# Attention block on one core: values and denominators side by side on TensorE, the tail's row operations parted, the tail's loads moved

## The reference

```python
mod = (silu(c) @ w_mod)                       # rows sa, ca, ga, sb, cb, gb for each batch
h = layernorm(x) * (1 + ca) + sa
q, k, v = split(h @ W_qkv + b_qkv)            # 16 heads of 32 channels
q, k = rope(q), rope(k)
p = softmax(causal(q @ k.T / sqrt(32)))
x = x + ga * ((p @ v) @ W_proj + b_proj)
h = layernorm(x) * (1 + cb) + sb
x = x + gb * (layernorm(h + outs) * ln_g + ln_b)
```

## Time and profile before

| | us |
|---|---|
| median of 3 runs | 3283.07 (3282.28 to 3283.45) |
| the profiled execution | 3289.78 |
| its span, first to last instruction | 3288.0 |
| PE busy | 3013.8 (92%) |
| DVE busy | 2501.4 (76%) |
| ACT busy | 1849.9 (56%) |
| POOL busy | 1588.9 (48%) |

### The profile page before, as it was taken

One profiled execution on the slowest core, in us unless ns is written; L12 is line 12 of the kernel. 1 busy time (PEld: TensorE's weight loads), 2 busy tenths in 40 slices (PEclk: granted clock), 3 DMA queues, 4 the chain that ended last, 5 costly groups with the idle time before them and its releaser, 6 DMA issues.

```text
span 3288.0 us, 59164 instructions
## 1 busy us (share of the span) xinstructions
PE 3013.8 (92%) x21664; PEld 1155.9 (35%) x21664; DVE 2501.4 (76%) x4214; ACT 1849.9 (56%) x3651; POOL 1588.9 (48%) x1586
## 2 busy tenths in 40 slices
PE   3799999999989999999998999999998999999896
PEld 1324343434343433434333242433324343242222
DVE  4697777777768788777877878777886878878477
ACT  3416565786655554785455555587545555455541
POOL 2303434482616465382644726365471645627355
PEclk8759999999999999999999999999999999999997
DMA  5403030413041220413113041311314122031122
GB/s 210 107 6 70 11 75 14 101 39 76 14 104 40 61 66 24 98 43 86 39 47 100 27 95 33 80 54 42 83 36 114 39 56 59 30 75 46 55 74 65
DMA packets 180875, 205.27 MB, mean 62 GB/s; under 512 B 21460, under 2 KB 137428, under 8 KB 179428
## 3 DMA queue, kind: packets, MB, share of 16 engines
q1 hardware_dynamic: 180584, 201.50, 23.4%
HBM read 114.09 MB, written 36.50 MB: 46 GB/s over the span
## 4 chain that ended last, share of the span: by engine, by line
PE 46%; issue 19%; DVE 16%; POOL 6%; POOLq 5%; DVEq 3%; ACT 3%; DMA 1%; SPq 1%; ACTq 1%
PE ring L1147 10%; PE ps_out L1197 9%; DVE mpart L902 9%; PE ps_scores L1183 7%; PE ps_scores L1121 5%; PE ps_den L1214 4%; PE ps_den L1220 3%; PE ring L1169 3%; POOL psum L529 3%; PE ps_scores L1133 2%; POOL psum L528 2%; DVE wk L948 1%; DVE dsum L918 1%; DVE wk L946 1%; POOLq L502 1%
## 5 line engine op out<-in xcount | busy, mean ns | idle before, releaser
L730 ACT ACTIVATE prob<-ps_scores 128x512 f32<-128x512 f32 (+3 forms) x2560 | 1257.8, 537 | 981.9 <-PE ps_scores L1186 477.2
L902 DVE TENSOR_REDUCE mpart<-ring 128x1 f32<-128x512 f32 (+3 forms) x2560 | 1403.1, 599 | 344.4 <-PE ring L1147 179.5
L1147 PE MATMUL ring<-qk 96*128 96x512 f16 (+3 forms) x2560 | 876.7, 365 | 73.6 <-DVE mpart L902 56.3
L1183 PE MATMUL ps_scores<-qk 98*128 98x512 f16 (+3 forms) x2560 | 867.2, 352 | 55.7 <-ACT prob L730 28.4
L528 POOL TENSOR_TENSOR psum<-prob 128x512 f32<-128x512 f32 x360 | 481.7, 1338 | 391.9 <-ACT prob L730 299.9
L1197 PE MATMUL ps_out<-prob,v 128*32 128x512 f32 (+3 forms) x5120 | 607.6, 547 | 0.0
L1147 PEld LDWEIGHTS ring<-qk 96*128 96x128 f16 x2560 | 236.1, 98 | 887.3 <-DVE mpart L902 625.2
L529 POOL TENSOR_TENSOR psum<-prob 128x512 f32<-128x512 f32 x360 | 483.4, 1343 | 0.0
L1183 PEld LDWEIGHTS ps_scores<-qk 98*128 98x128 f16 x2560 | 247.1, 99 | 370.1 <-ACT prob L730 215.7
L1121 PE MATMUL ps_scores<-hT,wg 128*128 128x512 f16 x1536 | 345.6, 382 | 3.5 <-POOL hT L519 3.5
L547 POOL TENSOR_TENSOR xs<-xs,bc 128x512 f32<-128x512 f32 x60 | 77.4, 1289 | 383.4 <-DMA xs<-in_L_attn_x_dram 382.1
(11 more groups left out here) (126 smaller groups left out, 2719.7 us busy)
## 6 DMA issues: line engine op xcount, KB each, us to landing
qk<-half SPq DMA_DIRECT2D x384, 128.0 KB, 3.6
turn<-in_rope_dram SPq DMA_DIRECT2D x64, 512.0 KB, 4.7
xs<-in_L_attn_x_dram SPq DMA_DIRECT2D x124, 256.0 KB, 2.8
attn_out_T<-ot SPq DMA_DIRECT2D x63, 256.0 KB, 2.2
otin<-attn_out_T SPq DMA_DIRECT2D x30, 512.0 KB, 4.8
out_dram<-x SPq DMA_DIRECT2D x60, 256.0 KB, 2.1
wg<-w_qkv_halves SPq DMA_DIRECT2D x16, 768.0 KB, 5.6
qk<-in_L_wmod_dram SPq DMA_DIRECT2D x1, 6144.0 KB, 26.8
```

Of the source, the lines that this page charges most:

```text
L730: act.activation(prob[:, s % 3, p, h % 2, 0:w], ps_scores[(HG * s + h) % NBK][:, 0:w], ACT.Exp, scale=SCALE).then_inc(exp_done, 1)
L902: dve.tensor_reduce(mpart[:, h, qt, kc:kc + 1], ring[use % NBK][:, 0:w], AX.X, ALU.max).then_inc(ring_free, 1)
L1147: mm = pe.matmul(ring[use % NBK][:, 0:w], qk[0:R, G % 2, 0, h, qt * P:(qt + 1) * P], qk[0:R, G % 2, 1, h, kc * QC:kc * QC + w], start=True ...
L1183: mm = pe.matmul(ps_scores[k % NBK][:, 0:w], qk[0:RM, par, 1, h, kt * P:(kt + 1) * P], qk[0:RM, par, 0, h, cq * QC + q0:(cq + 1) * QC], st ...
```

## The change

PE: V moves from place 2 to place 3 in every step, right ahead of D. The order becomes S0 U0 S1 U1 S2 U2 S3 V D U3 U4. DVE: of the two row operations of stages 2 and 4 only the first stays in its place; the second comes after the maxima of U2 and U3. U2's maximum also goes ahead of the reciprocals of parts 0 and 2, U3's ahead of those of parts 1 and 3. SP: the six rows of a new batch are loaded in chunk 0, and the first tail tile's load goes behind the rope load and behind the stacking of chunk 2's queries.

```diff
             def qkv(G, before, row_load, tail_load):
                 for c in range(NC_):
                     if c > 0:
                         stack_halves(G, c - 1, 1)
-                    if c == 2:
-                        tail_load()
                     if G < NG * B - 1 or c < NC_ - 1:
                         load_turn(NC_ * G + c + 1)
                     if c == 0 and before is not None:
                         maxima_rows(before, before % 2)
+                    if c == 0:
+                        row_load()
                     stack_halves(G, c, 0)
+                    if c == 2:
+                        tail_load()
                 stack_halves(G, NC_ - 1, 1)
...
+            def rows_load(b):
+                sp.wait_ge(tail_done, wait_value(NT * b))
+                sp.wait_ge(mod_st, 32)
+                sp.dma_start(bc[:], mod_d[b, 2:8, :].rearrange("(a m) n -> a m n", a=1).to_broadcast(
+                    [P, 6, C])).then_inc(bc_ld, 16)
+
             def tail_loads(b, t, xs_use, count):
                 Z = NT * b + t
-                if t == 0:
-                    sp.wait_ge(tail_done, wait_value(Z))
-                    sp.wait_ge(mod_st, 32)
-                    sp.dma_start(bc[:], mod_d[b, 2:8, :].rearrange("(a m) n -> a m n", a=1).to_broadcast(
-                        [P, 6, C])).then_inc(bc_ld, 16)
...
+                    def row_load():
+                        if 0 in tail.values():
+                            rows_load(b - 1)
...
                     dve.wait_ge(tail_rstd1, Z + 1)
                     dve.scalar_tensor_tensor(wk[:, i, :], x1[:, i, :], mv[:, i, 0:1], bc[:, 2, :], ALU.subtract, ALU.mult)
+                elif stage == 3:
                     dve.drain()
-                    dve.scalar_tensor_tensor(wk[:, i, :], wk[:, i, :], rstd[:, i, :], bc[:, 3, :], ALU.mult, ALU.add)
-                    dve.drain()
-                elif stage == 3:
                     dve.bn_stats(stats[:, i, :], wk[:, i, :])
...
                 else:
-                    tail_third(b, t)
+                    dve.wait_ge(tail_rstd2, Z + 1)
+                    dve.scalar_tensor_tensor(wk[:, i, :], wk[:, i, :], mv2[:, i, 0:1], bc[:, 4, :], ALU.subtract, ALU.mult)
+
+            def tail_second_row(b, t, stage):
+                i = t % 2
+                dve.drain()
+                if stage == 2:
+                    dve.scalar_tensor_tensor(wk[:, i, :], wk[:, i, :], rstd[:, i, :], bc[:, 3, :], ALU.mult, ALU.add)
+                else:
+                    dve.wait_ge(tail_x1_shift, NT * b + t + 1)
+                    dve.scalar_tensor_tensor(x1[:, i, :], wk[:, i, :], rstd2[:, i, :], xs[:, i, :], ALU.mult,
+                                             ALU.add).then_inc(tail_done, 1)
...
                                 tail_stage(b - 1, tail[s - 2 * stage], stage)
-                        out_parts(G, g, s, (0, 2), first, bool(own))
                         for u, h in units[2:3]:
                             unit_max(h, u, n)
                             n += 1
+                        out_parts(G, g, s, (0, 2), first, bool(own))
+                        for u, h in units[3:4]:
+                            unit_max(h, u, n)
+                            n += 1
+                        for stage in (2, 4):
+                            if s - 2 * stage in tail:
+                                tail_second_row(b - 1, tail[s - 2 * stage], stage)
...
-                            if place == (3 if s > 1 and STEPS[s - 1][1] == 0 else 2) and s > 0:
+                            if place == 3 and s > 0:
                                 values(G, par, s - 1, nxt)
-                            if place == 3 and s > 0:
                                 denominators(G, s - 1, nxt)
```

More of the change, by code:

```diff
@@ L359, in stack_halves, with qkv @@
                                  half[:, kind, a, :]).then_inc(stack_dma[kind], 16)
-            def qkv(G, before, tail_load):
+            def qkv(G, before, row_load, tail_load):
                 for c in range(NC_):
@@ L426, in body @@
                     else:
-                        qkv(NG * b + g + 1, NG * b + g, lambda: tail_load(FIRST_TAIL))
+                        qkv(NG * b + g + 1, NG * b + g, row_load, lambda: tail_load(FIRST_TAIL))
                     if not (last and g >= NG - 2):
@@ L440, in body @@
                             store_out(b - 1, tail[s - 9])
+                        if s + 2 in own and own[s + 2] == 0:
+                            rows_load(b)
                         if s + 2 in own:
@@ L467, in _ @@
             load_turn(0)
-            qkv(0, None, lambda: None)
+            qkv(0, None, lambda: None, lambda: None)
             load_group(1)
@@ L1035, in body @@
                         out_parts(G, g, s, (1, 3), first, bool(own))
-                        for u, h in units[3:]:
+                        for u, h in units[4:]:
                             unit_max(h, u, n)
```

## The result

The kernel after takes 3288.07 us (median of 14 runs, 3283.67 to 3291.99), the kernel before, run beside it on the same chip, 3281.03 (14 runs, 3277.34 to 3285.09). The ratio is 1.0022 [1.0015, 1.0030]: 7 us slower, where 62 us faster was forecast. The two profiled executions stand closer together: the span fell from 3288.0 to 3286.4, because the one of before lies 8.7 us above its later median and that of after (3288.19) does not. What follows goes group by group, and against more than one run of the same order.

A forecast was written before the change was run, and what follows sets the result against it. PE, busy 92% of the span, was taken to bound the kernel, with POOL nearly as hard in tail stretches. Terms -12 + 18 - 54 - 18 + 4 = -62 gave 3228, less 6.7 for the median: 3221 us, 8-in-10 range 3172 to 3268.

The forecast's parts named there:

- groups 0, 1, 3: Attention-only groups, PE idle 1.7 us only: V and D joined save 4 us a group, -12 in all.
- head groups: Groups 2, 6, 10: odd steps wait for the head's bank, other joins give back 2.4; +6 us each, +18.
- nine tail groups: Groups with tail tiles: joins and shorter waits for DVE give -6 us each, -54 (nothing to -10 each).
- loads: First projection phase of a new batch: rope load ahead of the tile removes waits, -18 us (-22 to -8).
- last group: No U between S0 and S3, so full-width steps wait on ACT: +0.17 in 21 steps, +4 us (-4 to +8).
- Joins where PE decides: Groups 0, 1, 3: each V-D join saves 0.24 us of PE, 24 joins a group, taken as -4 a group.
- Odd head steps: Groups 2, 6, 10: U2 waits for ACT to empty the head's bank, V and D behind it; +0.88 in 14 steps.
- stretches under POOL's pace: Tail-group stretches full of POOL's additions, half the joins: PE gains at most POOL's idle 8.1 us, taken as 2.
- joins outside: Tail-group joins outside the stretches full of POOL's additions: 13 at 0.24 us save 3.1 a group.
- waits for DVE: Tail groups: the 1.28 us before step 24's projection and some smaller waits go, 2 us a group.
- The first rival, POOL's pace: Locked ports and full POOL stretches leave 1 us a tail group in place of 6: -17, 3266 us; chance 0.14.
- Second rival, U2 too early: U2 ahead of V waits for its bank in every step with a D: +42 at w = 0.3, 3325 us; chance 0.11.

The follow-up runs named there:

- the rows alone: The kernel before with only DVE's parted row operations and earlier maxima: 3273.14 us, ratio 0.9976, 6.7 us faster.
- with POOL light: Kernels before and after, each with POOL's pair additions over 128 of 512 columns: 3210.82 and 3217.09 us.
- the tile's place mended: The kernel after with the first tail tile's load moved behind the stacking of chunk 2's keys: 3261.76 us, ratio to before 0.9945.
- the order alone: The kernel before with only the new place of V on PE: 3306.41 us, ratio 1.0077, 27 us slower.
- the loads alone: The kernel before with only SP's moved loads: 3278.04 us, ratio 0.9996.
- where it pays 3: After with selective V-D joins, statistics ahead of U3's maximum, later first tail tile load and addition, head tiles' loads ahead of columns and weights: 3223.09 us, ratio to before 0.9823.
- the three versions with the later tile: After with the first tail tile's load behind chunk 2's key stacking, alone or with two sets of further edits: 3261.76, 3238.11 and 3223.09 us.

## Why the prediction was wrong, step by step

The terms, forecast and as the profiles have them (the second from the same group lengths and step lengths as above):

| term | forecast | profile |
|---|---|---|
| groups 0, 1, 3 | -12 | -12.4 |
| head groups | +18 | +22.9 |
| nine tail groups, steps 2 to 39 | -54 | -15 |
| loads: steps 0 and 1 of tail groups, projection phases | -18 | +1.5 |
| last group | +4 | +2.7 |
| sum | -62 | about 0 |

The sum goes with the two profiles, whose spans differ by -1.6. The medians differ by +7, because the execution of before that was profiled is an unusually long one: its group 7 alone stands 5 above groups 11 and 14. So the -15 of the tail groups flatters the change; some 10 is likelier, an estimate from those three groups.

- *Joins where PE decides*: right for the group, 4.1 with 4 forecast. Of the 24 newly joined steps of group 1, 13 save 0.23 to 0.25, the size read from the earlier trace rows, and 130.7 us is the length in every run with all of these joins.
- *Odd head steps*: right in place and size. Step 27 of group 2 in after, for comparison with the earlier trace rows:

```profile
693.71 0.38 PE L1207 MATMUL ps_scores<-qk 98*128 98x512 f16 x1
695.30 0.39 PE L1171 MATMUL ring<-qk 96*128 96x512 f16 x1 [1.21 <-ACT x L773]
695.52 0.38 PE L1207 MATMUL ps_scores<-qk 98*128 98x512 f16 x1
695.84 1.07 PE L1221 MATMUL ps_out<-prob,v 128*32 128x512 f32 x8
696.72 1.04 PE L1238 MATMUL ps_den<-psum,ones 128*32 128x512 f32 x8
```

  U2 comes 2.47 after S0 (692.83) and D starts 0.88 behind V; such steps grew by 0.85, forecast 0.88. A head group grew by 7.6 on average, forecast 6. What was left out is that U3's maximum also moved ahead of the head's statistics (with the rows alone 0.68 in each of two steps).
- *The tail term, -6 a group*: this step failed, above all in the price of a join. The forecast's parts were the stretches under POOL's pace 2, joins outside 3.1 (13 at 0.24), waits for DVE 2, off again 1 for steps of few units. The five-tile groups got -1.8. The parted rows alone give -1.1, 0.83 of it in step 24: the wait there, which the forecast had gone, fell from 1.28 to 0.45, and in after to 0.69 (group 5):

```profile
1239.36 2.75 PE L1193 MATMUL ring<-wp,otin 128*128 128x512 f16 x12 [0.69 <-DVE mpart L911]
```

  The order on top of the rows gives only -0.8, where the joins less the short steps had been put at 4.1. From the rows alone to after, the steps that shrink sum to 3.7 and those that grow to 2.9. Seven of the 24 newly joined steps (7, 9, 15, 21, 27, 31, 39) save 0.24 or more, step 21 by no longer losing the 0.62 that the rows alone cost it; most narrow ones save from nothing to 0.19, some wide ones nothing. Of the growth, 1.4 is steps 4, 6, 28, 32 and 34, where by theory 4 S3 has lost V's cover (the trace of step 6 shows it), and 0.66 is step 17, which gives back what the parted rows had won there; step 2 grows by 0.45, and no run gives the cause. What the whole shortfall is due to stays open, since taking the growth out of four of these steps made the group no shorter. In groups 11 and 14, with six tiles, after gives +0.2 and -0.3 over these steps: steps 4, 16, 18, 28, 33 and 34 grow by 0.3 to 0.8, and steps 18 and 19 have half clock in part. The first rival, POOL's pace, came near to the tail's sum for a wrong reason: the stretches of the earlier trace rows are nearly as full of POOL in after (86 and 89%) as before (90 and 90%), yet with POOL light the change wins the same. The windows of after over about the same steps:

```profile
1192.30:1224.90 32.60, 30.81 (x200) 10.29 (x199) 29.66 (x50) 19.25 (x38) 27.93 (x25) 1.00 0.20 62
1242.20:1290.00 47.80, 45.36 (x263) 13.60 (x262) 41.26 (x66) 26.48 (x50) 42.48 (x37) 1.00 0.05 18
```

- *The loads, -18*: this step failed too, by a cost put at nothing. Step 0 gave 21 us back as computed. The prediction named the two stackings that the tile's loads now preceded, and that ACT awaits them within step 0, and put no price on it: step 1 took 20.5 us again, and two projection phases 2. What the prediction feared instead, the six rows pushing the rope table back, is not there (4.8 us of waits left); they lengthen two projection phases a little. With the tile's place mended the kernel is 26 us faster than after.
- *Second rival, U2 too early*: its mechanism showed where DVE's rows are whole (2.13 and 2.22 us in steps 21 and 35 of the order alone) and not in after (0.29 in step 21). The parted rows are what keeps it away, which the prediction counted as a gain of their own.
- *Last group*: the full-width step takes 3.25 (3142.39 - 3139.14), forecast 3.24, with the wait of the earlier trace rows in it; most such steps grew by 0.19, forecast 0.17. The narrow steps, put at nothing, grew by 0.06 or 0.07 each, and steps 1 and 31 fell by 0.88 and 0.68, so that the term came out at +2.7. PE in one full-width step of after:

```profile
3139.14 0.81 PE L1207 MATMUL ps_scores<-qk 98*128 98x512 f16 x3
3140.21 0.39 PE L1207 MATMUL ps_scores<-qk 98*128 98x512 f16 x1 [0.26 <-ACT prob L739]
...
3142.39 0.82 PE L1207 MATMUL ps_scores<-qk 98*128 98x512 f16 x3
```

What stays open, besides the tail groups' joins: why step 1 of groups 4 and 8 took anything from 5.2 to 7.9 us in the three versions with the later tile.

## What to carry over

An instruction between two others of one engine may be the cover of a wait that no profile shows yet: before moving it, look at what it stands between, and price each kind of step, not the mean step. A transfer moved ahead in a queue is late for someone else: list the next issues behind its new place and who awaits each, with the buffer that will be overwritten, and give each a price of its own. Try the parts of a change singly; here the order cost 27 us alone, the loads changed nothing, the rows won 7, and each part had a place where it paid.

## What the runs showed of the hardware

A wait of PE can cost twice: in or right behind some of them the granted clock falls to half (1.2 GHz) and stays there for 3 to 10 us, and whether it does differs between groups of one kernel and between kernels with the same wait. The 2.33 us before the projection of step 30 in six-tile groups is the clearest case. Group 14, the loads alone and then the parted rows alone:

```profile
3028.04 5.28 PE L1178 MATMUL ring<-wp,otin 128*128 128x512 f16 x12 [2.33 <-DVE mpart L911]
```

```profile
3025.13 2.75 PE L1184 MATMUL ring<-wp,otin 128*128 128x512 f16 x12 [0.49 <-DVE mpart L902]
```

Twelve products took 5.28 us behind the one wait, at a granted clock of 0.50 from 3026.79 to 3033.62, and 2.75 behind the other, at 1.00. In the six such steps with 2.33 us of wait (before and the loads alone, three groups each) the step took 8.96 to 8.97 three times and 10.65 to 11.45 three times, with half clock in these three; with the parted rows and V at its old place (the rows alone and where it pays 3), and 0.49 of wait, it took 7.12 to 7.13 in all six. To remove most of the 2.33 is so worth up to 4.3 (11.45 - 7.13). In the new wait of 1.60 in step 1 of group 11 the clock fell as well.
